# Both query stacks turned by DMA transposes, and the first key transposes issued ahead of the bulk of the loads

## What is computed

```
x = x + attention0(layernorm(x), ctx, mask)         # mask differs by batch
x = x + bitlinear_ffn(layernorm(x))                 # quantized weights and activations, 128 -> 512 -> 128
x = x + attention1(layernorm(x), ctx, mask1)        # one mask, per-head weights, output bias
x = x + moe(layernorm(x))                           # 8 experts 128 -> 256 -> 128, top 2, all computed
```

## Time and profile before

| | us |
|---|---|
| median of 3 runs | 222.78 (222.42 to 223.64) |
| the profiled execution, time | 223.34 |
| the profiled execution, span | 221.5 |
| busy in the span: PE | 195.2 (88%) |
| DVE | 162.5 (73%) |
| ACT | 134.7 (61%) |
| POOL | 88.2 (40%) |

### The profile page before, as it was taken

How to read it: one execution, slowest core, us unless ns; L and a number is a source line. 1 busy time by engine, 2 the same in 40 slices (tenths; PEclk the granted TensorE clock), 3 DMA queues, 4 the chain that set the end, 5 groups by cost and what they waited for, 6 DMA issues and landing times.

```text
span 221.5 us, 6113 instructions
## 1 busy us (share of the span) xinstructions
PE 195.2 (88%) x2114; PEld 160.9 (73%) x2114; DVE 162.5 (73%) x605; ACT 134.7 (61%) x377; POOL 88.2 (40%) x200
## 2 busy tenths in 40 slices
PE   2450787899999999999999999999999999999992
PEld 0230465566777766777789977978798999999992
DVE  1460598997999999999999999675746356564215
ACT  3320065678657978569787576985685565566440
POOL 9594036343432537254413583430106025523541
PEclk9999999999999999999999999999999999999999
DMA  5999532735342090516750000550000000000000
GB/s 168 357 355 242 115 60 41 131 63 93 70 85 43 3 176 16 98 35 62 99 98 0 1 15 4 95 98 0 3 0 6 12 3 13 3 12 12 15 0 24
DMA packets 39587, 15.09 MB, mean 68 GB/s; under 512 B 34179, under 2 KB 38659, under 8 KB 39302
## 3 DMA queue, kind: packets, MB, share of 16 engines
q1 hardware_dynamic: 38982, 14.00, 30.1%
q10 hardware_dynamic: 576, 0.72, 0.9%
HBM read 5.80 MB, written 0.52 MB: 29 GB/s over the span
## 4 chain that ended last, share of the span: by engine, by line
PE 69%; DVE 14%; issue 9%; DMA 3%; POOL 2%; ACT 1%; SPq 0%; DVEq 0%; ACTq 0%
PE ps_A L818 13%; PE ps_B L805 12%; PE ps_O L735 6%; PE ps_Q L689 5%; PE ps_A L656 5%; PE ps_A L658 5%; PE ps_B L673 4%; PE ps_B L671 4%; DMA x_sb<-in_x 3%; DVE mx L1034 3%; PE ps_O L743 2%; PE ps_X L705 2%; PE ps_A L814 2%; PE ps_P L717 1%; PE ps_O L753 1%
## 5 line engine op out<-in xcount | busy, mean ns | idle before, releaser
L1034 DVE TENSOR_REDUCE mx<-ps_A 128x4 f32<-128x512 f32 x64 | 42.7, 681 | 11.2 <-PE ps_A L658 11.1
L932 ACT ACTIVATE hid<-ps_B,b_sb 128x128 f32<-128x128 f32 x128 | 35.8, 379 | 20.0 <-PE ps_B L805 19.8
L883 ACT ACTIVATE probs<-ps_B 128x512 f32<-128x512 f32 x64 | 36.9, 605 | 9.3 <-PE ps_B L673 9.2
L656 PE MATMUL ps_A<-m_b,id_b 128*128 128x512 bf16 x64 | 25.3, 395 | 10.0 <-issue 9.6
L805 PE MATMUL ps_B<-mxT,w_sb 128*128 128x128 f32 x256 | 33.1, 278 | 0.0
L635 POOL TENSOR_TENSOR yc<-yc 128x512 f32<-128x512 f32 (+2 forms) x21 | 17.3, 823 | 36.4 <-DVE yc L1199 35.2
L818 PEld LDWEIGHTS ps_A<-w_sb,hid 128*128 128x128 f32 x256 | 31.1, 192 | 0.6
L818 PE MATMUL ps_A<-w_sb,hid 128*128 128x128 f32 x256 | 31.2, 275 | 0.0
L805 PEld LDWEIGHTS ps_B<-mxT,w_sb 128*128 128x128 f32 x256 | 30.4, 192 | 0.4 <-issue 0.4
L673 PEld LDWEIGHTS ps_B<-qmT,kblk 118*128 118x128 bf16 x256 | 19.8, 97 | 8.2
L658 PE MATMUL ps_A<-kblk,qT 112*128 112x256 bf16 x128 | 25.5, 281 | 0.0
(11 more groups left out here) (133 smaller groups left out, 399.0 us busy)
## 6 DMA issues: line engine op xcount, KB each, us to landing
w_sb<-in_m1T SPq DMA_DIRECT2D x1, 1024.0 KB, 6.7
w_sb<-in_m2T SPq DMA_DIRECT2D x1, 1024.0 KB, 7.8
m_i<-in_mask SPq DMA_DIRECT2D x1, 512.0 KB, 8.8
m0T_i<-in_mask0T SPq DMA_DIRECT2D x1, 512.0 KB, 9.5
out_y<-out_sb SPq DMA_DIRECT2D x8, 64.0 KB, 1.5
x_sb<-in_x SPq DMA_DIRECT2D x1, 448.0 KB, 7.5
ctx_sb<-in_ctxT ACTq DMA_DIRECT2D x1, 448.0 KB, 6.4
wf_sb<-in_wg SPq DMA_DIRECT2D x1, 256.0 KB, 8.4
```

What stands on the lines that cost most here:

```text
L656: pe.matmul(o[:, :].rearrange("p (h k) -> p h k", h=4), id_b[:, :], m, start=True, stop=False)
L883: ends(act.activation(probs[:, n % 2, 4 * i:4 * i + 4, :], psum("exp", n, i)[:, :].rearrange("p (h k) -> p h k", h=4), ACT.Exp, scale=ATTN ...
L932: ins = act.activation(hid[:, b % 2, 4 * i + c, :], psum("z", b, i)[:, c * P:(c + 1) * P], ACT.Relu, bias=b1_sb[:, 4 * i + c:4 * i + c + 1])
L1034: ends(dve.tensor_reduce(mx[:, n % 2, 4 * i:4 * i + 4], psum("max", n, i)[:, :].rearrange("p (h k) -> p h k", h=4), AX.X, ALU.max), "dve.max")
```

## The change

1. The two PE transposes of each unit, `qs` and `qb`, become DMA transposes issued by SP (new L575 and L583), eight blocks of 128x128 each. They write `qT` and `qmT` directly; ACT's two copies and the bank `ps_Q` go. The freed bank goes to `xT` and `q`, which now have two.
2. Rings: `qst` from three buffers to four, `qT` and `qmT` from two to three. At most two DMA transposes of one kind are in flight: each waits for the last but one to land.
3. The loads on SP are split. x, the constants and the masks of batches 0 and 1 come first; then the first key transpose; the rest follows behind the key transposes of units 0 to 3 (`later_loads`).
4. The clears of the first stacks move from POOL to DVE, the clear of `b2_p` behind the first key stack; ACT runs an Exp on one column before its first step; PE's two opening waits move to the steps that need them; some buffers are shared (`b2_sb` and `b2_f` with `yc`, `th` and `hr` with `wf_sb`).
5. `START`, `BIAS` and `ARRIVES` have new numbers, and `AFTER_KEYS` makes the steps that need the later loads wait in the plan for the key transposes before them. So the order changes on all engines.

```diff
+KSTACKS = 2
+QSLOTS = 4
+TSLOTS = 3
+MSLOTS = 3
+FLIGHTS = 2
...
-RING = {"A": 2, "B": 2, "P": 1, "X": 1, "Q": 1, "O": 1}
+RING = {"A": 2, "B": 2, "P": 2, "X": 1, "O": 1}
...
-    ("pe.qs", 1, "pool.ql"),
-    ("act.qs", 1, "pe.qs"),
-    ("pe.max", 4, "act.qs", "sp.ks"),
+    ("sp.qs", 1, "pool.ql"),
+    ("pe.max", 4, "sp.qs", "sp.ks"),
...
-    ("pe.qb", 1, "dve.m3"),
-    ("act.qb", 1, "pe.qb"),
-    ("pe.exp", 4, "act.qb"),
+    ("sp.qb", 1, "dve.m3"),
+    ("pe.exp", 4, "sp.qb"),
...
-START = (-36, -22, 2, -46, 42, 62, 14, 36, 63, 53, 102, 61, 36, 4, 44, -80)
+START = (-83, -9, 16, -15, 39, 18, 57, 33, 19, 7, 53, 67, 128, 84, 178, 123)
...
-            sp.dma_start(m0_i[:, :, :], mask0.rearrange("b q k -> q b k")).then_inc(s_mask[0], 16)
-            sp.dma_start(m0T_i[:, :, :], mask0T).then_inc(s_mask[1], 16)
...
+            def later_loads(n):
+
+                if n == 0:
+                    sp.dma_start(wo_sb[0][:, :], w0o).then_inc(s_wo, 16)
+                if n == 1:
+                    masks(1, 2, NB)
+                    for k, src in enumerate((wg, wu, wd)):
+                        sp.dma_start(wf_sb[:, k, :], src).then_inc(s_wf[k], 16)
+                if n == 2:
+                    sp.dma_start(m1_i[:, :], mask1).then_inc(s_mask1[0], 16)
...
+                if n == 3:
+                    sp.dma_start(w1_sb[:, :, :], m1T).then_inc(s_moe, 16)
+                    sp.dma_start(w2_sb[:, :, :], m2T).then_inc(s_moe, 16)
...
+            masks(0, 0, 2)
...
+                    later_loads(n)
+                if name == "qs":
+                    after(sp, "pool.ql", n)
+                    if n >= TSLOTS:
+                        after(sp, "pe.max", n - TSLOTS)
+                    if n >= FLIGHTS:
+                        wait_landed(sp, n - FLIGHTS, "qs")
+                    sp.dma_start_transpose(qT[:, n % TSLOTS, :, :], qst[:, n % QSLOTS, :, :].rearrange("p g c -> p (g c)")
+                                           ).then_inc(landed["qs"][n % FLIGHTS], 16)
+                if name == "qb":
+                    after(sp, "dve.m3", n)
+                    if n >= MSLOTS:
+                        after(sp, "pe.exp", n - MSLOTS)
+                    if n >= FLIGHTS:
+                        wait_landed(sp, n - FLIGHTS, "qb")
...
-            def stack(name, n, rows):
-
-                wait_free(pe, name, n)
-                o = psum(name, n)[:, :].bitcast(BF16)
-                for g in range(GROUPS):
-                    mm = pe.transpose(o[0:rows, g * P:(g + 1) * P], qst[:, n % 3, g, 0:rows], id_b[:, :])
-                ends(mm, "pe." + name)
...
-                    words("act.qs", qT[0:ROWS, n % 2, :, :], psum("qs", n)[0:ROWS, :])
...
+            zeros = lambda ap: dve.memset(ap.bitcast(F32), 0.0)
+            zeros(kst[:, 0, :, :, :]).then_inc(kst_zero, 1)
+            zeros(qst[:, 0, :, :]).then_inc(qst_zero, 1)
+            zeros(kst[:, 1, :, :, :]).then_inc(kst_zero, 1)
```

More of the change, by code:

```diff
@@ L292, in ready @@
             needs.append(("dve.dn", number[0, b], 0))
+        if name in AFTER_KEYS and b >= AFTER_KEYS[name][0]:
+            needs.append(("sp.ks", AFTER_KEYS[name][1], 0))
         if b == 0:
@@ L409, in build @@
         b1_sb = sb("b1_sb", [P, ZCH])
-        b2_sb = sb("b2_sb", [P, E * P])
-        b2_f = sb("b2_f", [P, E * P])
+        yc = sb("yc", [P, 2, E, P])
+        b2_sb, b2_f = [yc[:, i, :, :].rearrange("p e o -> p (e o)") for i in range(2)]
         b2_h = sb("b2_h", [P, E * P], BF16)
@@ L538, in _, with masks @@
-            sp.dma_start(b1_sb[:, :], mb1).then_inc(s_moe, 16)
-            sp.dma_start(gT_sb[:, :], gT).then_inc(s_moe, 16)
-            sp.dma_start(gb_sb[:, :], gb.partition_broadcast(P)).then_inc(s_moe, 16)
+            def masks(part, first, last):
+                sp.dma_start(m0_i[:, first:last, :], mask0[first:last].rearrange("b q k -> q b k")
+                             ).then_inc(s_mask[2 * part], 16)
+                sp.dma_start(m0T_i[:, first:last, :], mask0T[:, first:last, :]).then_inc(s_mask[2 * part + 1], 16)
@@ L834, in _ @@
             act.dma_start(ctx_sb[:, 1:NB, :], ctxT[:, 1:NB, :]).then_inc(s_ctx, 16)
+            act.wait_ge(half_ready, 1)
+            act.activation(warm[:, :], half[:, :], ACT.Exp)
             for name, n, i in order["act"]:
```

209 lines of the change are left out of this document (97 added, 112 removed).

## The result

The changed kernel takes **224.06 us** (median of 7, 223.32 to 224.57) against 222.42 for the kernel before on the same chip: ratio 1.0064, 95% interval 1.0036 to 1.0091. It is slower by a little over the half per cent that a measurement tells from no change. The forecast was 213.0 us (204 to 222); both its sign and its range missed.

The account below looks back on a forecast made before the run. Three limits in turn: a waiting start, a middle where PE and DVE tie, an end PE paces. 45 + 109.3 + 57.4 = 211.7 us of span; with 1.84 around it and 0.56 off for the median, 213.0 (204 to 222).

Parts of the forecast that it names:

- The first score at 14 to 15 us, unit 1's scores at 26 to 29: Start: first score matmul at 14 to 15 us instead of 23.43, then idle PE and DVE until unit 1's scores.
- The transpose: Each query DMA transpose takes 1.18 us of service and lands after about 3.1 us.
- The start, 45 us: Up to unit 1's first shifted score: 45 us against 42.97 before, a loss of 2 us.
- The queue's sum: Start: loads, transposes and gaps in the DMA queue up to unit 1's qmT transpose add up to 44.0 us.
- The middle, 109.3 us: From unit 1's first shifted score to the last row maxima: 109.3 us against 115.9 before.
- both give 109.3: Middle: PE's reduced work and DVE's floor each lead to 109.3 us.
- PE's 6.6 us: Middle: PE's work shrinks by 6.6 us, 11.3 of transposes gone less 4.7 net of work moved in.
- DVE's floor of 109.2: Middle: DVE's 106.1 us of busy time at 97% busy takes 109.2 us.
- The end, 57.4 us: After the last row maxima PE paces: 62.6 us less 4.7 moved forward less one group of 0.45.
- Rival (a): Start: loads and transposes overlap, unit 1's shifted scores start near 37 to 38; 7 us less, 206; chance 0.17.
- Rival (b): Query transposes' latency comes onto the path at 26 hops; slower if over 0.38 us each, 226 at 0.5; chance 0.17.
- Rival (c): DVE keeps the middle's pace: 2.7 us won there, 5.2 at the end, minus 2, giving 216.9; chance 0.17.

Follow-up runs that it names:

- experiment 14: Changed kernel with a useless four-block DMA transpose ahead of each of the 32 query transposes, waited for together with it: 242.37 us, ratio 1.0863.
- experiment 15: Changed kernel with a useless four-block DMA transpose of a blank tile behind each query transpose, waited for by nobody: 238.08 us, ratio 1.0698.
- experiment 1: Changed kernel with the experts' loads (2.1 MB) behind unit 6's key transpose instead of unit 3's: 225.28 us, ratio 1.0112.
- experiment 9: Changed kernel with the experts' loads in eight pieces of 0.25 MB, one behind each of the key transposes 3 to 10: 222.02 us, ratio 0.9972.
- experiment 5: Changed kernel with 22 useless matmuls ahead of unit 1's scores and 24 ahead of unit 0's output matmul: 224.86 us, ratio 1.0096.
- experiment 10: Kernel before with seven of the eight matmuls of each query transpose on PE left out: 219.45 us, ratio 0.9864.
- experiment 12: Kernel before with seven eighths of PE's query transposes and a quarter of DVE's row-maximum reduction left out: 216.25 us, ratio 0.9714.
- experiment 7: Changed kernel with the order's ranks (START and BIAS) of the kernel before, all else kept: 236.03 us, ratio 1.0619.
- experiment 16: Changed kernel with only four of the eight blocks turned in each query transpose: 222.00 us, ratio 0.9990.
- experiment 13: Changed kernel with each row maximum on DVE reading 96 of the 128 keys of a head: 221.63 us, ratio 0.9969.
- experiment 2: Changed kernel with the experts' loads issued from ACT's queue, behind ACT's key copies of unit 4: 221.92 us, ratio 0.9974.

## Why the prediction was wrong, step by step

**The first score at 14 to 15 us, unit 1's scores at 26 to 29**: 15.30 and 30.04. Nearly right.

**The transpose**, 3.1 us to landing: 2.8. Right. (The 1309 ns a block of the Trainium skill, VectorE: DVE Perf Modes, The three transpose paths, would be 10.5 us as an estimate for eight blocks one after another; the trace has eight landing in 2.8.) That throughput suffices held only as an average: by experiments 14 and 15, SP's list was already close to where each further 1.2 us costs 0.4 to 0.6.

**The start, 45 us**: measured 49.00. Two things failed. The queue's sum was too small: it had unit 1's qmT transpose landed at 44.0, and it was issued at 42.65 and landed at 47.55, 3.5 us later. Which of its terms was short, no run parts. And only this transpose was followed. Another one behind the same 2 MB, unit 4's key transpose, which nobody on PE needs yet, holds ACT's in-order list for 7.25 us, and with it unit 0's output matmul; that adds the last 1.5 us. Experiment 1 moves the loads and takes both away (start 43.91), experiment 9 too (43.56). Of the clock the forecast had only a slow first stretch of PE: the rows show 0.76 and 0.77 up to 49 us and half up to 53.3, behind waits of PE of 4.70, 5.55 and 5.89 us. Experiment 5 prices the last of them at 1.9 us in the middle.

**The middle, 109.3 us**: measured 116.6, the largest miss. The step that failed is "both give 109.3". The first of the two, PE's 6.6 us, valued a transpose group at its 0.45 us on PE's timeline. That was read from a stretch that PE paces; in most of the middle DVE was as full, and experiment 10, which takes seven eighths of the middle's 25 groups, measures their worth at 1.6 us, not 9.8. The second, DVE's floor of 109.2, took it that DVE could be at 97% all through. The new order puts 4.7 us of experts' work into the middle, onto PE, and PE is then the full engine from 105 us on. DVE's busy time in the middle is 106.0 us, as the forecast had it, but DVE is idle for 10.6 us: 7.8 behind 105, where PE is full, 1.8 up to 60, where the clock is low, and 1.0 between. At the measured worth of the relief the sum is 115.5 - 1.8 + 4.7 = 118.4; it came out 1.8 better, with 1.9 of low clock in it, and what made up for these isn't known. Two shares of a tie don't fall together because the sums of both allow it; it took the two reliefs in the same stretch, in experiment 12, to win 5.2 us.

**The end, 57.4 us**: 56.8. Nearly right, in the working too: behind the last maxima PE alone paces (52.71 of 56.70), so work moved away from there is won. But that work went into the middle, where PE is full as well. Middle and end together are 178.5 us before and 173.4 after; the 5.1 won are less than the 6.0 lost in the start. 5.1 us for 14.4 us of PE is the worth of the transposes in this kernel, with the latency, the clock and the order all in it.

**Rival (a)**, the queue isn't the limit of the start: refuted. The DMA share is 1.10 from 30 to 49 us, and with the 2 MB moved or split the start is 43.6 to 43.9, not 37 to 38. **Rival (b)**, latency on the path: not in its form. PE waits for a query transpose twice in the changed kernel, 5.5 us in the start and 1.0 in the middle, not at 26 hops. Yet its mechanism is near: what is sensitive is SP's order of issue (experiments 7, 9, 14, 15), and in experiment 16 half the blocks and 0.4 us less to landing gave some 2 us. By the number, slower than before, (b) came closest. **Rival (c)**, DVE keeps the pace: the nearest in mechanism. It gave 216.9 because it credited the end's 5.2 us without charging them to the middle, and because of the start. Its chance of 0.17 was too low: the profile showed DVE at 97% where the gain was to come.

What stays open: how the remaining loss of the middle divides between the order, SP's list and the tie. Experiments 13 (2.7 us), 16 (1.9) and 5 (1.9) each take a part away, and weren't combined. In the start it is open how much the chain through ACT costs without the other one.

## What to carry to other kernels

Where two engines are both full in a stretch, count work taken from one of them at a small part of its time (a sixth in experiment 10's middle) until something also relieves the other, and look at who paces where moved work lands. In an in-order queue follow every transfer behind a block of loads, also those that nobody seems to need yet: a buffer's next writer may stand ahead of the critical work on its own engine. Of the whole change the early key transpose was the part worth having, and it needed no other: with each load placed behind the transpose that can't wait, and ahead of the one that can, it gives 0.971.

## What the runs showed of the hardware

A DMA transpose of four blocks holds the issuing queue 1.19 us and lands in 2.3 to 2.5, one of eight blocks 1.24 and 2.8, one of sixteen 1.7 and 3.9: mostly a fixed price, about 0.12 us a block to landing on top. The edit of experiment 14 took the hold to shrink with the size, and it hardly does.

In experiment 5 useless matmuls in the place of a wait of 5.9 us ran at the lower clock until 48 us (granted 0.50), and it was back at 1.00 from 50, ahead of the useful work. They took 8.01 us, which is more than the slow stretch behind the wait cost.

Loads that stand ahead of a DMA transpose in the same queue delay it by their own service: behind 2 MB one landed 10.2 us after its issue (3.6 with nothing ahead, experiment 1), and 7.2 with the same loads in ACT's queue (experiment 2).
